# Turning an adjacency matrix into a mask: an accumulating transfer from GpSimd's queue in place of a VectorE pass

## The reference, cut to what matters

```
Wh     = einsum('bsf,hfd->bhsd', features, W)
scores = einsum('bhsd,bhtd->bhst', Wh, Wh) / sqrt(D)
scores = where(adj[:, None] > 0, scores, -9e15)
h      = einsum('bhst,bhtd->bhsd', softmax(scores), Wh)
```

## Time and profile before

| | |
|---|---|
| median of 3 runs | 2534.38 us (2531.88 to 2535.02) |
| the profiled execution | 2537.21 us, its span 2535.5 us |
| PE busy | 2281.9 us, 90% |
| DVE busy | 2173.3 us, 86% |
| ACT busy | 1944.8 us, 77% |
| POOL busy | 167.5 us, 7% |
| share of PE in the chain that ended last | 64% |

### The profile page before, as it was taken

One profiled execution on the slowest core, in us unless ns is written; L12 is line 12 of the kernel. 1 busy time (PEld: TensorE's weight loads), 2 busy tenths in 40 slices (PEclk: granted clock), 3 DMA queues, 4 the chain that ended last, 5 costly groups with the idle time before them and its releaser, 6 DMA issues.

```text
span 2535.5 us, 56744 instructions
## 1 busy us (share of the span) xinstructions
PE 2281.9 (90%) x23694; PEld 1528.0 (60%) x23813; DVE 2173.3 (86%) x4125; ACT 1944.8 (77%) x2161; POOL 167.5 (7%) x104
## 2 busy tenths in 40 slices
PE   3668999989999999999989899998989999998966
PEld 3557556575765658575665757656485765657341
DVE  3688799898988989898898989889898989989756
ACT  2758798787879878787987778788787878878714
POOL 0000001001000100100010010001001000100000
PEclk9788999999999999999999999999999999999978
DMA  6504133222323322232332123233222323101000
GB/s 129 134 18 118 42 85 77 62 74 43 102 68 85 83 65 64 43 101 68 85 84 66 62 43 101 68 85 76 60 77 42 102 68 85 45 33 52 9 17 9
DMA packets 192976, 172.80 MB, mean 68 GB/s; under 512 B 137168, under 2 KB 171088, under 8 KB 191696
## 3 DMA queue, kind: packets, MB, share of 16 engines
q1 hardware_dynamic: 191424, 135.61, 19.5%
q0 software_dynamic: 1296, 33.56, 6.5%
HBM read 151.78 MB, written 42.53 MB: 77 GB/s over the span
## 4 chain that ended last, share of the span: by engine, by line
PE 64%; DVE 14%; issue 9%; ACT 8%; DMA 3%; POOL 2%; SPq 1%; POOLq 0%; ACTq 0%; DVEq 0%
PE kp L821 15%; PE kp L804 10%; PE fp L707 9%; PE fp L646 9%; PE kp L797 6%; PE kp L752 3%; DVE weight L1317 3%; ACT ramp L994 3%; DMA shared<-shared 2%; DVE bstat L1127 2%; ACT weight L1037 2%; PE kp L749 2%; POOL bsmall L541 2%; PE fp L600 2%; PE fp L593 1%
## 5 line engine op out<-in xcount | busy, mean ns | idle before, releaser
L994 ACT ACTIVATE ramp<-s1row,tbig 128x1024 bf16<-128x1024 f32 x864 | 921.0, 1143 | 85.6 <-DVE weight L1317 85.5
L1037 ACT ACTIVATE weight<-kp,shift 128x1024 f32<-128x1024 f32 x512 | 543.9, 1114 | 196.2 <-PE kp L804 194.7
L1317 DVE TENSOR_TENSOR weight<-ramp,AT 128x2048 bf16<-128x2048 bf16 x512 | 609.6, 1221 | 75.9 <-ACT ramp L994 52.1
L821 PE MATMUL kp<-weight,w 128*33 128x512 f32 x2048 | 490.9, 600 | 9.5 <-ACT weight L1037 5.7
L707 PEld LDWEIGHTS fp<-vh_parts,weight 128*128 128x128 bf16 x8192 | 402.8, 100 | 130.5 <-DVE weight L1317 66.7
L707 PE MATMUL fp<-vh_parts,weight 128*128 128x102 bf16 x8192 | 431.9, 212 | 40.0 <-DVE vh L1325 24.7
L804 PE MATMUL kp<-shared 32*128 32x512 f32 x2048 | 298.0, 652 | 9.8 <-ACT weight L1037 7.5
L821 PEld LDWEIGHTS kp<-weight,w 128*33 128x33 f32 x2048 | 97.7, 110 | 321.4 <-issue 255.9
L646 PEld LDWEIGHTS fp<-features,weight 128*128 128x128 f32 x2048 | 234.9, 194 | 40.9 <-issue 40.3
L646 PE MATMUL fp<-features,weight 128*128 128x129 f32 x2048 | 240.7, 279 | 16.9 <-DVE weight L1228 16.9
L1456 DVE SCALAR_TENSOR_TENSOR weight<-AT,weight 128x1024 f32<-128x1024 bf16 x182 | 214.6, 1222 | 36.7 <-ACT weight L1037 36.7
(11 more groups left out here) (179 smaller groups left out, 2527.3 us busy)
## 6 DMA issues: line engine op xcount, KB each, us to landing
s1row<-s_rows_dram SPq DMA_DIRECT2D x128, 512.0 KB, 4.1
adj_bf_dram<-in_adj_dram POOLq DMA_DIRECT2D x15, 2048.0 KB, 13.7
x<-in_x_dram SPq DMA_DIRECT2D x16, 512.0 KB, 7.5
xfT<-s_row_dram SPq DMA_DIRECT2D x16, 512.0 KB, 3.6
shared<-shared SPq DMA_DIRECT2D x32, 256.0 KB, 3.5
out_dram<-elu SPq DMA_DIRECT2D x16, 512.0 KB, 4.5
adj_bf_dram<-in_adj_dram POOLq DMA_DIRECT2D x2, 1024.0 KB, 10.8
s_rows_dram<-weight SPq DMA_DIRECT2D x16, 32.0 KB
```

The lines of the kernel that those rows point to most:

```text
L821: last = pe.matmul(kp[side(h), 0, :], w3[:, (2 * J + x) * H3 + h, :], weight3[:, w % P_RING, x * HALF:(x + 1) * HALF], start=(J == 0 and x ...
L994: act.activation(ramp[:, u % R_RING, :], s1row[:, h % S_RING, :], ACT.Relu, bias=tbig1[:, jt, h:h + 1], scale=BIG).then_inc(ramp_ready.sem, 1)
L1037: act.activation(weight3[:, w % P_RING, :], kp[:, 1 + 2 * (w % 2):3 + 2 * (w % 2), :].rearrange("p a n -> p (a n)"), ACT.Exp, bias=shift3[ ...
L1317: dve.tensor_tensor(edges[:, u % B_RING:u % B_RING + 2, :], ramp[:, u % R_RING:u % R_RING + 2, :], AT[:, third, jt:jt + 2, :], ALU.min).th ...
```

## The change

The pass of VectorE is gone. GpSimd's queue issues a transfer in its place that adds a tile of -1 (`minus`, 128 x 256 bfloat16, read again for each of the 32 pieces of a partition) to the third of `AT`. It waits for the same semaphore, `sum2_made`. Its semaphore rises by 16 when it has landed. TensorE's wait stays; VectorE now waits for the transfer too, before the first of its own mask products of a graph. All five tables of the queues are changed. On GpSimd the order was `rstd2`, `rstd3`, `rstd_tail`, `adjacency`, `rstd0`, `rstd1`; it is now `rstd2`, `rstd3`, `mask3`, `rstd_tail`, `rstd0`, `rstd1`, `adjacency`. On SyncE, x and the turned adjacency stood ahead of all `sources`; now the first of the `sources` stands ahead of both.

```diff
+        minus = sb("minus", [P, 2 * P], BF16)
...
-        mask3_made = signal("mask3_made", 1)
+        mask3_made = signal("mask3_made", 16)
...
-            (dict(maxima1=93, maxima3=44, project0=[25, 31, 35], project1=91, project2=102, project3=42, scores3=[49,
-                 53, 56, 60, 65, 71, 75, 83, 85, 87, 90, 94, 98, 101, 104, 106], self2=0, self_weights=62, shift3=47,
-                 sources1=95, spread0=48, spread1=96, sum1=[17, 18, 23, 26, 28, 30, 37, 38], sum2=[1, 2, 5, 8, 9, 11,
-                 15, 16], top0=40, turn0=[19, 24], turn1=89, turn2=99, turn3=39, turn_back=29, unit0=[73, 74, 77, 78,
-                 79, 80, 81, 82], unit1=[3, 4, 6, 7, 10, 12, 13, 14, 20, 21, 22, 27, 32, 33, 34, 36, 41, 43, 45, 46,
+            (dict(maxima1=93, maxima3=45, project0=[29, 31, 34], project1=91, project2=102, project3=42, scores3=[50,
+                 54, 57, 62, 65, 71, 76, 83, 85, 87, 90, 94, 98, 101, 104, 106], self2=0, self_weights=49, shift3=48,
+                 sources1=95, spread0=44, spread1=96, sum1=[17, 21, 23, 25, 26, 30, 37, 38], sum2=[1, 3, 4, 8, 9, 13,
+                 15, 16], top0=41, turn0=[18, 24], turn1=89, turn2=99, turn3=39, turn_back=27, unit0=[73, 74, 75, 77,
+                 78, 79, 81, 82], unit1=[2, 5, 6, 7, 10, 11, 12, 14, 19, 20, 22, 28, 32, 33, 35, 36, 40, 43, 46, 47,
...
-                 ramps=[0, 1, -1, 2, 3, 4, -1, 5, 6, 8, 9, 11, 13, 14, 16, 17, 22, 23, 28, -1, 29, 30, -1, 33, 37, -1,
-                 40, 41, 44, 45], ramps_ahead=[94, 95], second2=91, self2=7, sources1=76, sum1=[19, 20, 24],
+            (dict(cut1=[81, 82], cut1_second=[86, 90], elu=62, exp3=[31, 32, 34, 35, 38, 39, 42, 43, 46, 47, 53, 54,
+                 60, 61, 63, 64, 65, 66, 68, 69, 71, 72, 74, 75, 78, 80, 84, 85, 88, 89, 92, 93], exps0=37, exps1=77,
+                 first2=87, out3=[48, 67, 83, 96], prepare0=49, project0=[16, 19, 22], project1=73, project3=26,
+                 ramps=[0, 1, -1, 2, 3, 4, -1, 5, 6, 8, 9, 11, 13, 14, 15, 20, 21, 23, 28, -1, 29, 30, -1, 33, 36, -1,
+                 40, 41, 44, 45], ramps_ahead=[94, 95], second2=91, self2=7, sources1=76, sum1=[17, 18, 24],
...
-                 finish0=83, finish1=73, finish3=24, head1=[7, 13, 22, 29, 40, 49, 56, 65], lengths3=34, low2=101,
-                 mask3=33, masked3=[57, 62, 63, 64, 69, 70, 71, 72, 80, 81, 86, 91, 93, 96, 99, 100], maxima1=88,
-                 maxima3=36, maximum0=45, most0=35, norm0=84, norm1=89, norm3=27, out2=15, prepare=74, ramps=[2, 9,
-                 37, 44, 52], relu2=21, residual3=50, rest2=98, shift0=58, shift3=38, shifts1=90, stats2=16, tail3=61,
-                 top0=28, top1=87, unit0=[66, 67, 68, 75, 76, 77, 78, 79], unit1=[0, 1, 3, 4, 5, 6, 8, 10, 11, 12, 14,
-                 17, 18, 20, 23, 25, 26, 30, 31, 32, 39, 41, 42, 43, 47, 48, 51, 53, 54, 55, 59, 60], z0=46),),
+            (dict(affine2=20, columns1=[91, 92], cut1=[94, 96], cut1_third=[100, 102], divide1=77, elu1=81,
+                 finish0=78, finish1=70, finish3=25, head1=[7, 13, 22, 28, 39, 48, 58, 62], lengths3=34, low2=101,
+                 masked3=[56, 57, 63, 64, 65, 66, 80, 82, 83, 84, 85, 90, 93, 95, 98, 99], maxima1=87, maxima3=36,
+                 maximum0=43, most0=32, norm0=79, norm1=88, norm3=27, out2=15, prepare=71, ramps=[2, 9, 35, 44, 51],
+                 relu2=21, residual3=50, rest2=97, shift0=52, shift3=38, shifts1=89, stats2=17, tail3=61, top0=30,
+                 top1=86, unit0=[67, 68, 69, 72, 73, 74, 75, 76], unit1=[0, 1, 3, 4, 5, 6, 8, 10, 11, 12, 14, 16, 18,
+                 19, 23, 24, 26, 29, 31, 33, 37, 40, 41, 42, 46, 47, 49, 53, 54, 55, 59, 60], z0=45),),
...
-            (dict(adjacency=3, rstd0=4, rstd1=5, rstd2=0, rstd3=1, rstd_tail=2),),
+            (dict(adjacency=6, mask3=2, rstd0=4, rstd1=5, rstd2=0, rstd3=1, rstd_tail=3),),
...
-            (dict(adjacency=1, far=6, out=10, sources=[2, 3, 4, 5, 7], sources_ahead=[12, 13, 14], spread_row=9,
-                 store_row=8, store_sources=11, x=0),),
+            (dict(adjacency=2, far=6, out=10, sources=[0, 3, 4, 5, 7], sources_ahead=[12, 13, 14], spread_row=9,
+                 store_row=8, store_sources=11, x=1),),
...
+            def layer3_mask(b, third):
+                if b == 0:
+                    pool.wait_ge(consts_made, 4)
+                pool.wait_ge(sum2_made.sem, sum2_made.of(b))
+                pool.dma_start(AT[:, third].rearrange("p t (c n) -> p (t c) n", n=2 * P),
+                               minus[:].unsqueeze(1).broadcast_to([P, T * T // 2, 2 * P]), accum_op=ALU.add) \
+                    .then_inc(mask3_made.sem, 16)
...
-            def layer3_mask(b, third):
-
-                dve.wait_ge(sum2_made.sem, sum2_made.of(b))
-                dve.tensor_scalar(AT[:, third], AT[:, third], -1.0, None, ALU.add).then_inc(mask3_made.sem, 1)
-
             def layer3_masked(b, third, v):
 
                 for w in (2 * v, 2 * v + 1):
                     _, n, J = unit3(w)
+                    if w == 2 * masks(b)[0]:
+                        dve.wait_ge(mask3_made.sem, mask3_made.of(b))
                     dve.wait_ge(exp3_ready.sem, exp3_ready.of(b, w + 1))
```

More of the change, by code:

```diff
@@ L390, in graph_stack @@
         ON_PE = [
-            (dict(maxima1=93, maxima3=44, project0=[25, 31, 35], project1=91, project2=102, project3=42, scores3=[49,
-                 53, 56, 60, 65, 71, 75, 83, 85, 87, 90, 94, 98, 101, 104, 106], self2=0, self_weights=62, shift3=47,
-                 sources1=95, spread0=48, spread1=96, sum1=[17, 18, 23, 26, 28, 30, 37, 38], sum2=[1, 2, 5, 8, 9, 11,
-                 15, 16], top0=40, turn0=[19, 24], turn1=89, turn2=99, turn3=39, turn_back=29, unit0=[73, 74, 77, 78,
-                 79, 80, 81, 82], unit1=[3, 4, 6, 7, 10, 12, 13, 14, 20, 21, 22, 27, 32, 33, 34, 36, 41, 43, 45, 46,
-                 50, 51, 52, 55, 58, 59, 63, 64, 66, 67, 68, 70], values3=[54, 57, 61, 69, 72, 76, 84, 86, 88, 92, 97,
+            (dict(maxima1=93, maxima3=45, project0=[29, 31, 34], project1=91, project2=102, project3=42, scores3=[50,
[3 more added lines that the diff above has]
+                 78, 79, 81, 82], unit1=[2, 5, 6, 7, 10, 11, 12, 14, 19, 20, 22, 28, 32, 33, 35, 36, 40, 43, 46, 47,
+                 51, 52, 53, 56, 59, 60, 61, 64, 66, 68, 69, 70], values3=[55, 58, 63, 67, 72, 80, 84, 86, 88, 92, 97,
                  100, 103, 105, 107, 108]),),
@@ L399, in graph_stack @@
         ON_ACT = [
-            (dict(cut1=[81, 85], cut1_second=[86, 90], elu=66, exp3=[31, 32, 35, 36, 38, 39, 42, 43, 47, 48, 52, 53,
-                 58, 61, 62, 63, 64, 65, 68, 69, 71, 72, 74, 75, 78, 79, 83, 84, 88, 89, 92, 93], exps0=34, exps1=77,
-                 first2=87, out3=[49, 67, 82, 96], prepare0=46, project0=[15, 18, 21], project1=73, project3=26,
-                 ramps=[0, 1, -1, 2, 3, 4, -1, 5, 6, 8, 9, 11, 13, 14, 16, 17, 22, 23, 28, -1, 29, 30, -1, 33, 37, -1,
-                 40, 41, 44, 45], ramps_ahead=[94, 95], second2=91, self2=7, sources1=76, sum1=[19, 20, 24],
-                 turn0=[10, 12], turn1=70, turn2=80, turn3=25, unit0=[50, 51, 54, 55, 56, 57, 59, 60], wide3=27),),
+            (dict(cut1=[81, 82], cut1_second=[86, 90], elu=62, exp3=[31, 32, 34, 35, 38, 39, 42, 43, 46, 47, 53, 54,
[3 more added lines that the diff above has]
+                 40, 41, 44, 45], ramps_ahead=[94, 95], second2=91, self2=7, sources1=76, sum1=[17, 18, 24],
+                 turn0=[10, 12], turn1=70, turn2=79, turn3=25, unit0=[50, 51, 52, 55, 56, 57, 58, 59], wide3=27),),
@@ L406, in graph_stack @@
         ]
         ON_DVE = [
-            (dict(affine2=19, columns1=[92, 94], cut1=[95, 97], cut1_third=[102, 103], divide1=82, elu1=85,
-                 finish0=83, finish1=73, finish3=24, head1=[7, 13, 22, 29, 40, 49, 56, 65], lengths3=34, low2=101,
-                 mask3=33, masked3=[57, 62, 63, 64, 69, 70, 71, 72, 80, 81, 86, 91, 93, 96, 99, 100], maxima1=88,
-                 maxima3=36, maximum0=45, most0=35, norm0=84, norm1=89, norm3=27, out2=15, prepare=74, ramps=[2, 9,
-                 37, 44, 52], relu2=21, residual3=50, rest2=98, shift0=58, shift3=38, shifts1=90, stats2=16, tail3=61,
-                 top0=28, top1=87, unit0=[66, 67, 68, 75, 76, 77, 78, 79], unit1=[0, 1, 3, 4, 5, 6, 8, 10, 11, 12, 14,
-                 17, 18, 20, 23, 25, 26, 30, 31, 32, 39, 41, 42, 43, 47, 48, 51, 53, 54, 55, 59, 60], z0=46),),
+            (dict(affine2=20, columns1=[91, 92], cut1=[94, 96], cut1_third=[100, 102], divide1=77, elu1=81,
[5 more added lines that the diff above has]
+                 19, 23, 24, 26, 29, 31, 33, 37, 40, 41, 42, 46, 47, 49, 53, 54, 55, 59, 60], z0=45),),
@@ L537, in _ @@
                                pattern=[[-1, P]], channel_multiplier=1).then_inc(consts_made, 1)
+            pool.memset(minus[:], -1.0).then_inc(consts_made, 1)
             def rstd(var_ready, rstd_ready, small, b, n):
@@ L575, in step @@
                     load_adjacency(n + 1)
+                if k is not None and s == at["mask3"]:
```

(3 more changed lines are left out.)

## The result

The changed kernel takes 2628.3 us (median of 4 runs, 2626.07 to 2630.23) against 2533.13 for the kernel before, run beside it (2531.32 to 2535.02): a ratio of 1.0375, 95% interval 1.0357 to 1.0393. That is 95 us slower, where I forecast 16 us faster, and 53 us above the upper end of my range. The profiled execution has a span of 2625.6 us.

The account below looks back on a forecast made before the run. TensorE was taken to set the pace from the first score product on, leaving only the stretch before it to shorten. Reordering gave 15 x 1.1 = 16.5 us, pass and transfer 0: from 2534.4 to 2518 us, range 2500 to 2575.

Parts of the forecast that it names:

- it lands at 1296.3, ahead of need: GpSimd's mask transfer, issued about 1281.3, takes 15 us; about 17.8 us are free before the scores start.
- What the change adds: Prediction's part on the added 2 MB transfer on GpSimd's queue: 15 us taken, between bounds of 9.2 and 23.7.
- rival (c): Mask in time but sharing engines with the far transfer, which lands up to 2 us later: 2548 us; chance 0.07.
- (b): TensorE's first score product waits for a late mask transfer: 2567 us at 21 us, 2608 at 23.7; chance 0.24.
- The pass stood in a hole: VectorE's mask pass filled idle time before lengths, which waits for ScalarE's copy of w; removal alone taken as 0.
- The turn of x3 comes with norm3, and the stall before the third projection goes: On TensorE, the turn, 1.13 us late, follows norm3's end within 0.2 us; the 1.38 us projection stall disappears.
- The new orders give some 16 us: Reordering starts everything behind x3's turn sooner, 1.1 us in each of 15 sections: 16.5 us.
- The moved loads cost nothing: Adjacency load on GpSimd's queue, x and transpose on SyncE's: all arrive before need, costed at 0.
- GpSimd's hold makes nobody late: GpSimd's next step, rstd_tail, starts 33 us later, so even holding it for the whole transfer delays nothing.
- Rival (e): VectorE blocks GpSimd's descriptor writing, making the transfer some 3.5 us longer, 18.5 us: 2528 us; chance 0.05.
- a hole of 1.5 us ahead of lengths: On VectorE, with the pass gone, about 1.5 us of idle time expected before lengths in the new orders.

Follow-up runs that it names:

- e7: Changed kernel with the transfer at the same place adding in rows of 4096 bytes, from a row of -1 in DRAM: 2525.43 us, ratio 0.9973.
- e4: Changed kernel with the transfer moved first in GpSimd's section, ahead of rstd2: 2523.95 us, ratio 0.996 to the kernel before.
- e9: Changed kernel, transfer in place, but masked products read zeros and TensorE waits for the transfer only at the ninth pair of scores: 2626.73 us, ratio 1.0358.
- e8: Changed kernel with 24 products that nobody reads on TensorE ahead of its wait for the mask: 2594.49 us, ratio 1.0237.
- e6: Changed kernel with the transfer writing zeros over the same rows instead of adding -1, so nothing is masked: 2527.14 us, ratio 0.997.
- e5: Old order tables with the transfer first on GpSimd's queue in place of VectorE's pass: 2535.67 us, ratio 1.0007 to the kernel before.
- e3: Changed kernel with neither VectorE's pass nor the transfer, so no mask is made: 2524.22 us, ratio 0.9958.
- e11: Changed kernel with the transfer ahead of rstd2, and the adjacency load and SyncE's first steps back at their old places: 2527.53 us, ratio 0.9969.
- e1: Changed kernel's new orders with VectorE's pass put back ahead of lengths in place of the transfer: 2554.46 us, ratio 1.008.

## Why the prediction was wrong

**The step that failed** is "it lands at 1296.3, ahead of need", in *What the change adds*, and with it the small price of rival (c). Two terms of it were mis-sized and one was missing:

- *The transfer's length.* I took 15 us, by the nearest row, between bounds of 9.2 and 23.7; it is 20.2. That row, the adjacency load, moves its 2 MB in some 76 packets (1296 for 17 transfers), the mask in 4112; with 528 packets (e7) it is 16.1 us. Alone this would have cost a fraction of the loss: the mask lands at 1341.1, and by e4's 4.68 us from the far issue to the product, that product would have started at 1334.45 + 4.68 = 1339.1. Waiting for the mask would then cost 2 us a section, 15 x 2 = 30 us over e4, or 20 us over the kernel before (an estimate, without what the clock would take); the change cost 95.
- *What the overlap does to the other transfer.* I let the far transfer land "up to 2 us later". By the landings on record, from its issue to its landing and summed over the 15 sections that have such a wait, it is 135.3 us, in e4 67.8 us: 67.5 us, or 4.5 us a section; the last graph adds 3.1. e9 shows that this doesn't go through the mask.
- *TensorE's clock after the long wait*, which I had no term for. The clock lost in the 8 us from the weight load of each first product, (1 - granted) x 8, is 37.6 us over the 15 windows and 8.4 in e4, where only 5 of the 15 show a fall: 29.2 us. e8 measured 33.8 for all of it.

Together 67.5 + 3.1 + 29.2 = 99.8 of the 104.4 us between the changed kernel and e4; 4.6 stay open. Rival (c) had the mechanism and the place, at a chance of 0.07 and a seventh of the price; I had made (b) the slow case, and a wait of the score product on the mask was what I told the reader to look for. In the view of TensorE's products it never came: all 15 are released by the far transfer. In rival (b), 15 x 2.1 is 31.5 us and not 33, which moves nothing.

The Trainium skill (Collectives: The Full Stack, "The bandwidth ceiling: the fold count and why AG ≠ RS ≠ AR") says that an adding transfer reads twice and runs at half a copy's rate. The direction agrees: with as many packets the write takes 11.8 us and the adding transfer 16.1, and of the engines' time, without the loads' 6.5%, 11.0 - 6.5 = 4.5% (e6) and 13.7 - 6.5 = 7.2% (e7), a factor of 1.6 and not 2. My estimate by it was 16.4 us, 3.8 short of the 20.2 for these rows. That the 4096-byte rows take 16.1 is chance: the estimate was made from the price of 512-byte rows.

**Steps that held.**
- *The pass stood in a hole* of the old orders: e5 is at 1.0007, and lengths waits there for w.
- *The turn of x3 comes with norm3, and the stall before the third projection goes.* In the changed kernel:

```profile
1325.19 2.14 DVE L1156 TENSOR_SCALAR x<-yb,bsmall 128x128 f32<-128x128 f32 x8
```

```profile
1321.76 0.68 PE L635 MATMUL fp<-rhs,xfT 128*128 128x130 f32 x4
...
1327.39 1.09 PE L605 MATMUL kp<-ident,x 128*128 128x128 f32 x8 [0.37 <-DVE x L1156]
```

 norm3 ends at 1327.33 and the turn starts at 1327.39, 0.06 us behind, where it was 1.13; the projection no longer has the wait of 1.38.
- *The new orders give some 16 us.* Without the mask's harm a section is 146.5 us (e3 and e4; from 999.82 to 1146.34 in e4, first product to first product), against 146.1 forecast, and e4 is 10.4 us faster than the kernel before where I said 16.5: the term was right in kind and 6 us too large. Part of the 1.1 us comes back elsewhere in the section.
- *The moved loads cost nothing*: e11. *GpSimd's hold makes nobody late*: 3.2 us each time, with `rstd2` waiting for VectorE behind it in e4.
- Rival (e): no sign of it. The issue takes 3187 to 3255 ns in every section, whatever VectorE does, and the transfer is as long in e4, where it runs beside other work of VectorE (20.5 us), as in the change.

**A step that was wrong without moving the total:** I expected a hole of 1.5 us ahead of lengths in the new orders. It is 0.38:

```profile
1332.74 1.22 DVE L1439 TENSOR_TENSOR yb<-w 128x1024 f32<-128x1024 f32 x1 [0.38 <-ACT w L926]
```

 The hole before was 2.21 us, from the pass's start at 1291.90 to lengths at 1294.11. Of it 1.10 go because lengths comes sooner behind `norm3` (5.41 us in place of 6.51): that is the very gain of the reordering. And 0.62 go to two small operations of layer 0 (`most0`, 1330.51 to 1331.13), which the new table has ahead of lengths; my count of the pieces between `norm3` and lengths left them out. So in the new orders the removed pass is worth 30 us (e1 against e3), the clock's part in e1 included. Removing it and reordering belong together: each alone gives nothing (e5) or a loss of 0.8% (e1).

## What to carry to other kernels

A transfer that takes work off an engine is to be judged not by whether it lands in time, but by which small, urgent transfer is issued while it moves: here two transfers of 256 KB on the critical path were held up by the 2 MB, 4.5 us a section. Send the large one as soon as its input is free, ahead of other steps in its queue, and look in the trace for overlap with whatever the critical chain itself sends. And add to the price of a new wait on TensorE what the clock takes after it.

## What the runs showed of the hardware

- An adding transfer of 2 MB within SBUF in rows of 512 bytes makes one packet for each row (4112 a transfer) and takes 20.2 us; a plain write in the same rows makes 528 and takes 11.8, and adding in rows of 4096 bytes (from DRAM) 528 and 16.1. GpSimd is held for the issue for 3.2, 1.75 and 1.33 us.
- A small transfer issued into a large one can take twice its time: with 6.6 us of the mask's time to go, on the mean, the far transfer took 9.0 us from issue to landing in place of 4.5 (e4), and landed 1.8 to 3.3 us after the mask. Its first packet went out 2.8 us (median) behind its issue in place of 1.1; in the section shown the mask moved 838 packets in the 2.55 us behind that issue, and SyncE's queue none. Whether the size of the packets does this or only the length of the overlap stays open.
- After 5.3 to 6.7 us of idleness TensorE's granted clock fell in all 15 sections (0.65 to 0.84 on the mean of the 8 us behind the wait); after 1.3 to 1.8 us it did so in 5 of 15 (e4), and with the wait filled but for 0.3 to 1.4 us in none (e8).
